# New order in the slots of a transformer block, normalisation of late chunks on ScalarE, and identity products in the prologue

## The reference

```
x = x + attn_a(layernorm(x))   # 16 heads of 64, q k v with biases, causal softmax, Wo, bo
x = x + ffn(layernorm(x))      # 128 -> 512, relu, -> 128
x = x + attn_b(layernorm(x))   # one head of 128, scores x Wqk x^T, alibi term, causal
x = x + ffn(layernorm(x))      # the same weights again
```

## Time and profile before

| | us |
|---|---|
| runs | 642.22, 647.32, 646.46 (median 646.46) |
| profiled execution | 647.31 |
| its span, first to last instruction | 645.0 |
| PE busy | 565.8 (88%) |
| DVE busy | 481.3 (75%) |
| ACT busy | 457.8 (71%) |
| POOL busy | 397.0 (62%) |

### The profile page before, as it was taken

One profiled execution on the slowest core, in us unless ns is written; L12 is line 12 of the kernel. 1 busy time (PEld: TensorE's weight loads), 2 busy tenths in 40 slices (PEclk: granted clock), 3 DMA queues, 4 the chain that ended last, 5 costly groups with the idle time before them and its releaser, 6 DMA issues.

```text
span 645.0 us, 16576 instructions
## 1 busy us (share of the span) xinstructions
PE 565.8 (88%) x6230; PEld 414.0 (64%) x6230; DVE 481.3 (75%) x1450; ACT 457.8 (71%) x869; POOL 397.0 (62%) x376
## 2 busy tenths in 40 slices
PE   1668998978999999999999999999799998799697
PEld 1534766645666666766666676666588776577575
DVE  6446878877887787878778887887248799678774
ACT  3447887757878887888888888888745685156375
POOL 3275787856777887788778878888920142045410
PEclk9868999979999999999999999999999999689799
DMA  9422243222322323234233333340754000000001
GB/s 229 98 49 51 51 107 75 66 64 62 96 63 83 91 76 100 58 100 108 51 98 77 90 86 74 85 107 3 246 183 169 0 2 1 0 1 3 1 16 51
DMA packets 35327, 47.88 MB, mean 74 GB/s; under 512 B 10776, under 2 KB 16688, under 8 KB 35248
## 3 DMA queue, kind: packets, MB, share of 16 engines
q1 hardware_dynamic: 33136, 46.29, 26.3%
q10 hardware_dynamic: 2112, 0.54, 0.4%
HBM read 12.21 MB, written 9.44 MB: 34 GB/s over the span
## 4 chain that ended last, share of the span: by engine, by line
PE 35%; ACT 22%; issue 16%; DVE 14%; POOL 10%; DMA 2%; SPq 0%; POOLq 0%; ACTq 0%; DVEq 0%
POOL p_hl L1534 9%; ACT p L975 8%; ACT p_hl L976 7%; PE psum L479 5%; PE psum L481 5%; PE psum L480 4%; PE psum L523 3%; ACT v_all L921 3%; DVE v_all L1116 3%; DVE xn L1094 2%; PE psum L578 2%; PE psum L579 2%; PE psum L558 2%; PE psum L560 2%; PE psum L559 2%
## 5 line engine op out<-in xcount | busy, mean ns | idle before, releaser
L1534 POOL TENSOR_TENSOR p_hl<-p,p_hl 128x512 f16<-128x512 f32 x288 | 326.0, 1161 | 90.5 <-ACT p_hl L976 87.3
L1126 DVE CUSTOM_DVE_ANT_0 max_junk<-psum,mask_s 128x1024 bf16<-128x1024 f32 (+7 forms) x256 | 190.0, 753 | 62.1 <-issue 57.6
L975 ACT ACTIVATE p<-psum 128x512 f32<-128x512 f32 x288 | 179.4, 623 | 16.7 <-PE psum L581 13.4
L976 ACT ACTIVATE p_hl<-psum 128x512 f16<-128x512 f32 x288 | 181.2, 629 | 0.0
L523 PE MATMUL psum<-k_hh,q_hl 128*128 128x512 f16 (+3 forms) x384 | 108.2, 338 | 31.0 <-DVE maxima L1126 30.7
L558 PE MATMUL psum<-v_all,p_hl 128*128 128x65 f16 x1152 | 125.5, 193 | 3.6 <-POOL p_hl L1534 3.6
L559 PE MATMUL psum<-v_all,p_hl 128*128 128x64 f16 x1152 | 125.6, 193 | 0.0
L578 PE MATMUL psum<-q_hl,k_hh 128*128 128x512 f16 (+3 forms) x384 | 125.1, 330 | 0.3 <-DVE q_hm L1133 0.2
L560 PE MATMUL psum<-v_all,p_hl 128*128 128x65 f16 x1152 | 125.1, 195 | 0.0
L579 PE MATMUL psum<-q_hm,k_l 128*128 128x512 f16 (+3 forms) x384 | 123.0, 329 | 0.0
L558 PEld LDWEIGHTS psum<-v_all,p_hl 128*128 128x128 f16 x1152 | 107.9, 99 | 11.9 <-POOL p_hl L1534 4.0
(11 more groups left out here) (184 smaller groups left out, 1131.8 us busy)
## 6 DMA issues: line engine op xcount, KB each, us to landing
k_hh<-st_hi SPq DMA_DIRECT2D x64, 128.0 KB, 2.4
o_scratch<-o_sb SPq DMA_DIRECT2D x16, 512.0 KB, 3.1
o_in<-o_scratch SPq DMA_DIRECT2D x4, 2048.0 KB, 7.9
k_l<-st_lo SPq DMA_DIRECT2D x32, 128.0 KB, 2.4
q_hl<-st_hi SPq DMA_DIRECT2D x32, 128.0 KB, 2.3
q_hl<-st_lo SPq DMA_DIRECT2D x32, 128.0 KB, 2.3
q_hm<-st_hi SPq DMA_DIRECT2D x32, 128.0 KB, 2.3
x_sb<-in_L_attn_a_x SPq DMA_DIRECT2D x4, 256.0 KB, 4.1
```

The lines of the kernel that those rows point to most:

```text
L975: nc.scalar.activation(p32[:, ring_at(u, r), :], src, ACT.Exp, scale=SCALE_A).then_inc(exp_done, 1)
L976: nc.scalar.activation(p_hl[:, u % 2, 0, BANK * r:BANK * (r + 1)], src, ACT.Exp, scale=SCALE_A).then_inc(phi_done, 1)
L1126: nc.vector.tensor_tensor_reduce(out=max_junk[:, n % 2, 0:cols], in0=max_banks(j, 0, cols), in1=mask_s[:, S - cols:S], scale=1.0, scalar=- ...
L1534: nc.gpsimd.tensor_tensor(p_hl[:, u % 2, 1, cols], p32[:, ring_at(u, r), :], p_hl[:, u % 2, 0, cols], ALU.subtract)\
```

## The change

- **Slot order.** PE runs the output steps as 0, 1, then one each between the tiles and scores (2 behind tile 1, 3 behind tile 2, 4 and 5 behind tile 5, 6 behind tile 6, 7 and 8 behind tile 7). Scores 0 and 1 stand together ahead of tile 1. ACT takes the second projection behind exponentials 2 instead of 0. DVE takes `outputs(0)` between takes 1 and 2, `value_low` behind the take of tile 5 and `outputs(1)` behind the row write.
- **Late chunks.** Statistics in slots 1 and 2 (behind take 0), `rstd` and two new small products (`chunk_shift`: -mean x rstd) on POOL in slots 2 and 3, normalisation by ACT (`late_norm`) in slots 4 and 5, turn, high and low part in slots 5 and 6. `chunk_low` stands ahead of take 6.
- **Prologue.** 154 products of `ident_b` with itself into bank 5, which nothing reads (`idle_products`). Projections 4 and 5 stand among the tiles of head 0, the product of `Wo` ahead of these. The loads of the last two chunks of `x` stand ahead of the feed-forward weights. PE waits for all four value copies of ACT before the tiles. Low part 3 stands behind `gain_v` on DVE.

The diff, cut:

```diff
@@ -356,7 +358,7 @@
-        def late_chunk(u, step=4):
+        def late_chunk(u, step=3):
@@ -400,12 +402,12 @@
             sp.dma_start(bo_sb[:, :], bo.unsqueeze(1)).then_inc(bo_in, 16)
+            load_x(2)
+            load_x(3)
...
             sp.dma_start(b2_sb[:, :], b2.unsqueeze(1)).then_inc(ffn_in, 16)
-            load_x(2)
-            load_x(3)
@@ -546,6 +548,7 @@
                             pe.wait_ge(v_one, 1)
+                            pe.wait_ge(bo_done, 1)
@@ -614,48 +617,56 @@
                 products(0)
+                products(1)
                 maximum(0)
-                products(1)
                 project(0)
                 scores(u, 0)
+                scores(u, 1)
                 maximum(1)
-                scores(u, 1)
+                products(2)
                 scores(u, 2)
                 project(1)
                 maximum(2)
-                products(2)
                 products(3)
-                products(4)
-                products(5)
-                maximum(3)
                 scores(u, 3)
                 scores(u, 4)
+                maximum(3)
                 scores(u, 5)
                 value_unit()
                 maximum(4)
-                products(6)
                 maximum(5)
+                products(4)
+                products(5)
                 scores(u, 6)
                 maximum(6)
+                products(6)
                 if late_chunk(u) is not None:
                     pe.wait_ge(v_lo_done, units_after(u))
                     turn_chunk(late_chunk(u))
+                scores(u, 7)
+                maximum(7)
                 products(7)
-                maximum(7)
                 products(8)
-                scores(u, 7)
                 rows()
                 scores(u, 8)
+            def idle_products(n):
+
+                for _ in range(n):
+                    nc.tensor.matmul(bank(5)[:, 0:P], ident_b[:, :], ident_b[:, :], start=True, stop=True)
+
             pe.wait_ge(bias_in, 48)
-            pe.wait_ge(ident_ready, 1)
+            pe.wait_ge(ident_ready, 2)
             nc.tensor.transpose(bank(MAXB)[:, 0:3 * OB], b_rows[:, :], ident[0:3 * OB, 0:3 * OB]).then_inc(bt_full, 1)
             turn_chunk(0)
+            idle_products(8)
             turn_chunk(1)
+            idle_products(8)
             pe.wait_ge(sq_done, 4)
             pe.wait_ge(ones_ready, 1)
             nc.tensor.matmul(bank(MAXB + 1)[:, 0:4], ones[:, :], sums[:, 0:4], start=True, stop=True).then_inc(fro_full, 1)
+            idle_products(32)
             pe.wait_ge(first_lo, 2)
@@ -664,27 +675,28 @@
                 piece(n, FIRST_BANKS[n])
+            idle_products(12)
...
-
-            for n in range(4, 6):
-                pe.wait_ge(piece_lo, n)
-                piece(n, MISC)
+            pe.wait_ge(wo_in, 16)
+            for k in range(OB):
+                last = nc.tensor.matmul(bank(6)[:, 0:1], wo_raw[:, k, :], b_cols[:, 2, k:k + 1], start=(k == 0), stop=(k == OB - 1))
+            last.then_inc(bo_full, 1)
+
+            pe.wait_ge(v_hi_done, FIRST_UNITS)
+            idle_products(24)
...
             for n in range(QT):
+                if n:
+                    idle_products(10)
                 max_tile(0, n)
-                if n == 3:
-
-                    pe.wait_ge(wo_in, 16)
-                    pe.wait_ge(piece_lo, 6)
-                    for k in range(OB):
-                        last = nc.tensor.matmul(bank(MISC)[:, 0:1], wo_raw[:, k, :], b_cols[:, 2, k:k + 1], start=(k == 0), stop=(k == OB - 1))
-                    last.then_inc(bo_full, 1)
-            pe.wait_ge(bo_done, 1)
+                if n in (1, 2):
+                    pe.wait_ge(piece_lo, n + 3)
+                    piece(n + 3, MISC)
@@ -899,6 +911,16 @@
+            def late_norm(n):
+                act.wait_ge(shift_done, n - LATE_CHUNKS[0] + 1)
+                act.wait_ge(xt_full, n - 1)
+                for j in range(CT):
+                    tile = CT * n + j
+                    last = nc.scalar.activation(xn[:, n % 2, j, :], x_sb[:, tile, :], ACT.Identity, bias=shift[:, tile:tile + 1],
+                                                scale=rstd[:, tile:tile + 1])
+                last.then_inc(xn_ready, 1)
@@ -950,9 +972,8 @@
                 value_high(m, V_BANKS[m])
-                if m == 1:
-                    for n in range(4, 6):
-                        piece_high(n)
+            for n in range(4, 6):
+                piece_high(n)
@@ -983,9 +1004,11 @@
                 exponentials(u, 0)
-                project(1)
                 exponentials(u, 1)
                 exponentials(u, 2)
+                project(1)
+                if late_chunk(u, 2) is not None:
+                    late_norm(late_chunk(u, 2))
                 exponentials(u, 3)
@@ -1168,27 +1191,25 @@
                 maximum(0)
+                if late_chunk(u, -1) is not None:
+                    first_stats(late_chunk(u, -1))
                 project(0)
                 maximum(1)
+                outputs(0)
                 maximum(2)
                 project(1)
                 maximum(3)
-                outputs(0)
                 maximum(4)
+                maximum(5)
                 if unit_in(u) is not None:
                     value_low(unit_in(u))
-                maximum(5)
+                if late_chunk(u) is not None:
+                    chunk_low(late_chunk(u))
                 maximum(6)
                 maximum(7)
-                if late_chunk(u) is not None:
-                    chunk_low(late_chunk(u))
-                outputs(1)
                 if u + 1 < HEADS:
                     max_rows(u + 1)
-                if late_chunk(u, 1) is not None:
-                    first_stats(late_chunk(u, 1))
-                if late_chunk(u, 3) is not None:
-                    chunk_norm(late_chunk(u, 3))
+                outputs(1)
@@ -1265,23 +1286,23 @@
             norm_v()
-            for n in range(2, 4):
-                piece_low(n, FIRST_BANKS[n])
+            piece_low(2, FIRST_BANKS[2])
             gain_v()
+            piece_low(3, FIRST_BANKS[3])
             dve.wait_ge(inv_done, 2)
             first_low(2)
             for which in range(3):
                 rest_scale(which)
-            for n in range(4, 6):
-                piece_low(n)
             dve.wait_ge(tri_ready, 2)
             for n in range(QT):
                 take_max(0, n)
+                if n in (1, 2):
+                    piece_low(n + 3)
                 if n == 5:
                     dve.wait_ge(bo_in, 16)
                     dve.wait_ge(bo_full, 1)
-                    nc.vector.tensor_tensor(bo_all[:, :], bank(MISC)[:, 0:1], bo_sb[:, :], ALU.add).then_inc(bo_done, 1)
+                    nc.vector.tensor_tensor(bo_all[:, :], bank(6)[:, 0:1], bo_sb[:, :], ALU.add).then_inc(bo_done, 1)
             dve.wait_ge(diag_ready, 1)
@@ -1490,6 +1511,14 @@
+            def chunk_shift(n):
+                cols = slice(CT * n, CT * (n + 1))
+                nc.gpsimd.tensor_scalar(shift[:, cols], mean_var[:, cols, 0], -1.0, None, ALU.mult).then_inc(mean_turned, 1)
+                pool.wait_ge(mean_turned, n - LATE_CHUNKS[0] + 1)
+                pool.wait_ge(rstd_done, n + 1)
+                nc.gpsimd.tensor_tensor(shift[:, cols], shift[:, cols], rstd[:, cols], ALU.mult).then_inc(shift_done, 1)
@@ -1537,8 +1566,9 @@
                     low(u, r)
-                    if r == 4 and late_chunk(u, 2) is not None:
-                        chunk_rstd(late_chunk(u, 2))
+                    if r == 4 and late_chunk(u, 0) is not None:
+                        chunk_rstd(late_chunk(u, 0))
+                        chunk_shift(late_chunk(u, 0))
```

More of the change, by code:

```diff
@@ L155, in hybrid_block @@
     minus_half = sb("minus_half", [P, CT], F32)
+    shift = sb("shift", [P, TILES], F32)
     ident = sb("ident", [P, P], F32)
@@ L285, in hybrid_block @@
         bn_done, aggr_done, eps_done, rstd_done = sem("bn_done"), sem("aggr_done"), sem("eps_done"), sem("rstd_done")
+        mean_turned, shift_done = sem("mean_turned"), sem("shift_done")
         xn_ready, xt_full, xt_hi_done, xt_lo_done = sem("xn_ready"), sem("xt_full"), sem("xt_hi_done"), sem("xt_lo_done")
```

## The result

The changed kernel took 608.57 us (median of 4 runs, 606.81 to 613.79), the kernel before beside it 644.34 (4 runs, 642.04 to 647.32): ratio 0.9455, 95% interval 0.9391 to 0.952. The forecast was 617 in a range of 608 to 629, so the result lies at the range's lower end. Repeated later with more runs, the ratio was 0.9452 [0.9422, 0.9482].

A forecast was written before the change was run, and what follows sets the result against it. The slot was taken as PE's own work plus one wait, 0.62 us ahead of the 128-column tiles. 647.3 - 23.0 (slots 1 to 28) - 6.2 (prologue, slot 0) - 1.2 (end of slots) = 616.9, forecast 617, range 608 to 629.

The forecast's parts named there:

- Slots 1 to 28: Slots 1 to 28: 28 x 12.20 + 6.3 = 347.9 us against 370.9, a gain of 23.0.
- slots 29 and 30: End of the slots: POOL's subtractions end them; 0 to 2.2 us gained, 1.2 taken.
- margin of 0.1 us: Walk of the new slot order: no PE wait is left, but four margins are 0.1 us or less.
- they add up to 12.15: Plain slot: PE's pieces of work, read start to start, sum to 12.15 us; 12.20 was taken for the slot.
- the removed wait is worth 28 x 0.58: Slots 1 to 28: removing PE's wait ahead of the 128-column tile saves 0.58 us in each of 28 slots.
- rival C: Rival, chance 0.07: PE's busy time in the slots hides waits in projections and values; 0.3 given back, 608 us.
- A: Rival, chance 0.13: a margin breaks, tile 1 waits 0.3 us in every slot, 28 x 0.3 = 8.4; 625 us.
- D: Rival, chance 0.03: the second projection waits on ACT behind exponentials, values wait 1.8 us, slot period 14.0; 667 us.
- E: Rival, chance 0.05: the wait only moves from tile 7 to the values, the slot stays 12.78 us; 633 us.
- B: Rival, chance 0.10: the prologue gains nothing, PE stays at 1.2 GHz or the products are in the way; 623 us.
- Late chunks: Slots 1 to 6: moved statistics, normalisation on ACT and turning cost 6.3 us in total, against 12.7 before.
- Prologue and slot 0: Before slot 1: `q_hm` written at 54.3 instead of 60.55, 6.2 us gained; about nothing if the clock stays 0.5.

The follow-up runs named there:

- experiment with `value_low` alone: The kernel before with only `value_low` on DVE moved behind the take of tile 5: 632.39 us, ratio 0.9789.
- prologue run by itself: The changed kernel's prologue (orders, `bo`, identity products) in front of the slots of the kernel before: 638.05 us, ratio 0.991 against the kernel before.

## Why the forecast was near, and which step failed

The total was forecast 8 us too high (617 against 608.57). Slots 1 to 28 gained 7.4 us more than forecast, slots 29 and 30 lost 2.7 against it, and the sum started from 647.31, 3 us above the median of the kernel before. So 617 is near in part because errors cancel.

**Slots 1 to 28: right mechanism, wrong size.** The wait ahead of tile 7 went, no margin of 0.1 us broke, and nothing replaced the wait. The failed step is "they add up to 12.15", and with it "the removed wait is worth 28 x 0.58". The pieces named there, added up from the starts of all products in the 21 plain slots before, give 11.99: output products 3.28 (without the wait), tiles 1.99, two projections 1.59, scores 4.13, values 0.89, turned maxima 0.11. The 12.15 is not their sum but PE's busy time of 12.16, which I took as work. The rows of the kernel before around the wait (last product ahead of it, then the weight load of tile 7; tile 7 itself started at 263.94) show what is wrong with that:

```profile
263.12 0.20 PE L560 MATMUL psum<-v_all,p_hl 128*128 128x65 f16 x1
263.93 0.10 PEld L523 LDWEIGHTS psum<-k_hh,q_hl 128*128 128x128 f16 x1 [0.74 <-DVE maxima L1126]
```

That product starts at 263.12 and tile 7 at 263.94, 0.82 us later. With no wait the next product starts 0.03 us after such a one. So the wait costs 0.78, while the idle column says 0.62: it counts from the modelled end of a product 0.20 long, most of which would overlap the next one. Averages of all starts in the plain slots give the same: from an output product to tile 7 817 ns before, 34 ns with `value_low` moved. 12.78 - 0.78 = 12.00; another 0.045 went with the new order. I can't give that to one kind of product, since with other neighbours some distances grew and others shrank. 28 x (12.20 - 11.955) = 6.9 us, of the 7.4 by which this term was short: 4.5 for the wait's price (0.16 a slot), 1.3 for the 0.045, and 1.1 for the 0.04 that I had added for margins. The experiment with `value_low` alone repeats it on the other wait: 0.09 idle, 0.26 paid, and 12.78 - 0.78 + 0.26 = 12.26 is its slot, as measured (257.47 us for 21 slots).

That is rival C, which had a chance of 0.07 and named 608; it was right that busy time hid part of a wait and wrong about the place: by starts a projection takes 0.84 us now against 0.79 before, and a value unit 0.82 against 0.89. That its number is the measured one is in part luck, since its 0.3 a slot stood for another saving. A, D and E fell with the plain slot of 11.95; B fell with the prologue run by itself.

**Late chunks: right.** Forecast 6.3 us over plain slots, measured 340.46 - 28 x 11.955 = 5.7. The four ACT operations took 1.69 (1.5 taken): the estimate of 0.39 for one fits the distance of their starts (0.385), while each is 0.54 long, and slot 5 is the long one (14.66). Rows of it: the operations, and the two PE waits behind them.

```profile
113.14 1.69 ACT L920 ACTIVATE xn<-x_sb,shift,rstd 128x128 f32<-128x128 f32 x4
118.04 0.66 PE L492 MATMUL psum<-ident,xn 128*128 128x128 f32 x4 [0.79 <-DVE v_all L1139]
121.05 0.27 PE L540 MATMUL psum<-ident,maxima 128*8 128x128 f32 x1 [1.07 <-DVE maxima L1149]
```

The clock of 0.83 in that part of the kernel before is gone with the wait of 3.98 us ahead of it.

**Prologue and slot 0: right at full clock.** `q_hm` of slot 1 was at 54.54 (second profile), 54.3 forecast. On the way the first projection was later than forecast, 19.76 against 18.4, behind DVE's `w_lo`, and PE made up for most of it by tile 0 (31.72, forecast 31.2). In the first profile the row write came at 57.46. Three rows of that profile show where the clock rose and fell: the batch of 32 identity products (0.11 us apart at first, 0.056 after the first few, where PE stood idle before), `bo`'s products (1.84 us against 3.52), and the batch behind them.

```profile
16.09 2.21 PE L656 MATMUL psum<-ident_b 128*128 128x128 bf16 x32
28.22 1.84 PE L686 MATMUL psum<-b_cols,wo_raw 128*128 128x1 f32 x16
30.33 2.74 PE L656 MATMUL psum<-ident_b 128*128 128x128 bf16 x24 [0.27 <-ACT v_all L943]
```

And of the second profile, the last of them and tile 0:

```profile
30.37 1.51 PE L656 MATMUL psum<-ident_b 128*128 128x128 bf16 x24 [0.27 <-ACT v_all L943]
31.72 0.59 PE L525 MATMUL psum<-k_hh,q_hl 128*128 128x512 f16 x2
```

Both profiles have the same pause of 0.27 us there, and in the first the clock was 0.5 from 30.3 to 33.7. 24 products take 2.74 us at 1.2 GHz and 1.51 at 2.4; 1.2 of the 1.6 us between the two prologues are there. The rest of the difference is slot 0 (12.79 at 0.87, 11.45 at 1.00). Slot 0 opened on POOL's `wv_lo`, as forecast:

```profile
40.68 3.59 POOL L1551 TENSOR_TENSOR w_lo<-w_raw,w_hi 128x768 fp32r<-128x768 f32 x2 [8.80 <-ACT w_hi L979]
46.23 0.59 PE L525 MATMUL psum<-k_hh,q_hl 128*128 128x512 f16 x2 [1.69 <-POOL wv_lo L1551]
```

I had given the falling clock one end of the range and no share of the forecast. The runs say it comes and goes from execution to execution: of the nine profiles of kernels with such products in the prologue, six have a stretch at 1.2 GHz near 30 to 35 us, two of these another from 47 to 51, and three have none; slot 1's row write lies between 54.14 and 57.77.

**Slots 29 and 30: wrong sign.** I had POOL end them; PE's waits did. With no projections and values between the tiles, the new order asks for tiles 1, 2 and 4 before the takes ahead of them are done. Slot 29's waits:

```profile
401.01 0.55 PE L525 MATMUL psum<-k_hh,q_hl 128*128 128x512 f16 x2 [0.39 <-DVE maxima L1149]
402.76 0.50 PE L525 MATMUL psum<-k_hh,q_hl 128*128 128x512 f16 x2 [0.28 <-DVE maxima L1149]
405.70 0.55 PE L525 MATMUL psum<-k_hh,q_hl 128*128 128x512 f16 x2 [0.50 <-DVE maxima L1149]
```

1.17 us a slot, where the old order has 0.58. The old order put back gave 10.63 again.

## What to carry to other kernels

Where a wait of PE is to be removed, take its price from the starts of the products on either side of it, less the distance of the same pair where nothing waits, and not from the idle column: here the two were 0.78 and 0.62, over 28 slots 4.5 us. An order that is right for slots with filler work between dependent steps should be walked again for the slots that lack it. And before a profile's prologue or last stage is explained, a second profile of the same program tells which of its microseconds are the clock's.

## What the runs showed of the chip

**A DVE operation waits for POOL's.** Of the kernel before, DVE's four normalising operations of slot 6 are in the earlier trace rows; POOL's row under them is

```profile
127.87 4.49 POOL L1534 TENSOR_TENSOR p_hl<-p,p_hl 128x512 f16<-128x512 f32 x4
```

and in the experiment with the late normalisation on DVE the first two of the four, and POOL's:

```profile
106.35 1.46 DVE L1115 TENSOR_SCALAR xn<-x_sb,mean_var,rstd 128x128 f32<-128x128 f32 x2
106.32 1.16 POOL L1563 TENSOR_TENSOR p_hl<-p,p_hl 128x512 f16<-128x512 f32 x1
```

The first DVE operation is 1.21 us long and ends 0.08 after POOL's one that had begun 0.03 before it; the next takes 0.33 with POOL idle. In slot 6 of the kernel before each of the four began beside a fresh operation of POOL and took 1.07 to 1.19, and each ended 0.08 after that one. So the price of the form is 0.33, or what is left of POOL's operation and 0.08 where that is longer; 4.40 us was four such starts, and 2.0 is one. By the Trainium skill, page "SBUF — State Buffer", section "SBUF: two separate sides", a VectorE operation in a two-port mode and a GpSimd operation lock a shared port pair for the whole instruction. The trace agrees in that the DVE operation ends only behind POOL's; in which mode it ran, no row shows. ACT's same work took 537 to 549 ns each beside the same POOL.

**The clock of one program is not one number.** Between two profiles of the changed kernel PE ran at 1.2 GHz for a part of 30 to 51 us and for more of the stage from 508 to 536 in the one than in the other (means 0.965 and 0.984). The spans differ by 6.7 us; nothing in the program differed. The products that nothing reads made the whole program 4 to 6 us shorter when they stood in the prologue, and gained nothing behind the slots.
